# Two heads in 32 output rows, feature sums over two heads, key sums in PSUM, a shorter stage behind each chunk

## The reference

```python
h = rmsnorm(layernorm(x), norm_w);  q, k, v = h @ Wq, h @ Wk, h @ Wv          # 16 heads of 8
q_phi, k_phi = taylor(q @ Wqf), taylor(k @ Wkf)        # 1, 16 linear, 136 quadratic terms
# linear branch, chunks of 128 tokens with a running state (kv, ksum)
A = (qb . kb) * causal;  y = A @ vb + qb @ kv;  z = A.sum() + qb @ ksum;  lin = y / (z + 1e-6)
kv += kb.T @ vb;  ksum += kb.sum()
win = softmax(q . k / sqrt(8) over the last 65 tokens) @ v
x = x + (layernorm(x) + concat(lin, win) @ Wout)
# experts: top 2 of 8, weights by softmax of the two logits
x = x + sum_e combine[e] * (silu(g) * l) @ W3[e],   g, l from (xn @ W1[e]) * (xn @ W2[e])
```

## Time and profile before

| | |
|---|---|
| median of three runs | 486.39 us |
| the profiled execution | 485.23 us, its span 483.5 us |
| TensorE busy | 421.5 us, 87% |
| VectorE, ScalarE, GpSimd busy | 313.9, 215.2, 184.3 us |
| mean granted TensorE clock | 0.949 of 2.4 GHz |

### The profile page before, as it was taken

How to read it: one execution, slowest core, us unless ns; L and a number is a source line. 1 busy time by engine, 2 the same in 40 slices (tenths; PEclk the granted TensorE clock), 3 DMA queues, 4 the chain that set the end, 5 groups by cost and what they waited for, 6 DMA issues and landing times. The chain is left out here.

```text
span 483.5 us, 15295 instructions
## 1 busy us (share of the span) xinstructions
PE 421.5 (87%) x5093; PEld 294.4 (61%) x5093; DVE 313.9 (65%) x1289; ACT 215.2 (45%) x566; POOL 184.3 (38%) x320
## 2 busy tenths in 40 slices
PE   0887899999999999999999983299999999999930
PEld 0455677777777777777877762045555555555510
DVE  5475555777877778777787766446666666666614
ACT  1456455556455555555555540034444444434410
POOL 5254424435555455554545633202222222222220
PEclk9999899999999999999999995589999999999975
DMA  7548975445645555432222900211111111111008
GB/s 199 134 128 165 213 140 98 121 128 149 165 101 127 141 147 157 110 77 55 65 64 65 278 11 22 64 50 36 41 43 34 30 40 41 34 32 35 18 28 237
DMA packets 91630, 46.19 MB, mean 96 GB/s; under 512 B 56410, under 2 KB 89852, under 8 KB 91554
## 3 DMA queue, kind: packets, MB, share of 16 engines
q1 hardware_dynamic: 88562, 40.49, 34.3%
q0 software_dynamic: 2272, 4.46, 2.9%
q10 hardware_dynamic: 720, 0.26, 0.2%
HBM read 33.67 MB, written 11.98 MB: 94 GB/s over the span
## 5 line engine op out<-in xcount | busy, mean ns | idle before, releaser
L1303 POOL DMA_INDIRECT results<-qas,mrowid x39 | 38.3, 983 | 123.2 <-ACT qas L853 123.2
L1284 POOL TENSOR_SCALAR_AFFINE_SELECT amat<-amat 128x512 f32<-128x512 f32 x64 | 42.4, 662 | 100.2 <-ACT amat L793 99.6
L1076 DVE TENSOR_REDUCE mrow<-ps 128x4 f32<-128x512 f32 x64 | 44.0, 688 | 55.1 <-PE ps L585 55.1
L723 PE MATMUL ps<-wgl,rest 128*128 (+1 forms) x156 | 75.2, 605 | 2.9 <-DVE hT L1173 2.2
L806 ACT ACTIVATE pmat<-ps 128x512 f32<-128x512 f32 x64 | 38.2, 597 | 69.0 <-PE ps L640 69.0
L793 ACT ACTIVATE amat<-ps 128x512 f32<-128x512 f32 x64 | 38.2, 597 | 31.3 <-PE ps L597 31.3
L1173 DVE TENSOR_TENSOR hT<-ps,kv_tok 128x512 f32<-128x512 f32 x39 | 27.0, 691 | 26.6 <-PE ps L723 15.9
L723 PEld LDWEIGHTS ps<-wgl,rest 128*128 128x128 f32 x156 | 27.1, 193 | 25.5 <-issue 25.4
L708 PE MATMUL ps<-w,rest 128*128 (+1 forms) x78 | 41.9, 620 | 0.0
L640 PE MATMUL ps<-identb,mneg 128*128 128x128 bf16 x512 | 39.6, 220 | 0.0
L853 ACT ACTIVATE qas<-rest,mweight 128x128 f32<-128x128 f32 x39 | 15.7, 402 | 50.0 <-DVE rest L1190 50.0
(11 more groups left out here) (164 smaller groups left out, 921.7 us busy)
## 6 DMA issues: line engine op xcount, KB each, us to landing
qa_parts<-wgl SPq DMA_DIRECT2D x12, 256.0 KB, 3.5
ks<-k_parts SPq DMA_DIRECT2D x32, 96.0 KB
qas<-qa_parts SPq DMA_DIRECT2D x32, 96.0 KB
xin<-routed SPq DMA_DIRECT2D x39, 72.0 KB, 1.9
ks<-k_parts SPq DMA_DIRECT2D x32, 64.0 KB
qas<-qa_parts SPq DMA_DIRECT2D x32, 64.0 KB
w<-in_W SPq DMA_DIRECT2D x2, 1024.0 KB, 6.0
wgl<-in_Wg SPq DMA_DIRECT2D x2, 1024.0 KB, 6.1
```

The source lines that it names most:

```text
L723: t = mm(ps[:, GL, :], zxT[:, k % 2, s, :], rhs(wgl[:, bass.ds(e, 1), s, :]), start=(s == 0), stop=(s == 1))
L1076: v.tensor_reduce(mrow[:], ps[:, SQ, :].rearrange("p (a k) -> p a k", k=CH), AX.X, ALU.max).then_inc(max_done, 1)
L1284: q.affine_select(out=amat[:, u % 2], in_=amat[:, u % 2], compare_op=ALU.is_ge, fill=0.0, base=0, pattern=[[0, 4], [1, CH]], channel_multi ...
L1303: q.indirect_dma_start(results, bass.IndirectOffsetOnAxis(mrowid[:, m:m + 1], 0), yw[:, m, :], None, bounds_check=RESULTS - 1, oob_is_err= ...
```

## The change

Two heads h and h+4 of a group of eight now share 32 output rows: the tiles `v1` and `state` are laid out so that a read of 32 columns finds the first head's nine values at 0 and the second's at 16, and zeros elsewhere. Both heads' products are added in PSUM, so a bank takes two units. ScalarE copies it every second unit, `linT` and `winT` have half as many blocks, and four transposes in unit 0 of `post` bring back both branches (eight in two units before). The normalisation is one pass over 32 head slots; `Wout` is reordered on the host to fit.

The feature sums run as two matmuls over 256 columns (two heads at once) in place of four over 128. The key sums of a sequence stay in PSUM (144 columns of the KV bank) and accumulate there; VectorE masks them into one of two state tiles, one operation per unit. The last chunk of each sequence computes no key sums, key features or cross products.

`post` has its transposes of results in unit 1 and its projection in unit 2. Two passes follow the last chunk in place of three: routing of chunks 14 and 15 is done in unit 3 of the same pass as its logits. Waits by `settle` in the attention loop are gone. The core of the diff (old code as above where left out):

```diff
+SLOTW = 288
...
-        v1 = sb("v1", [CH, 2, 2, H, 32])
-        state = sb("state", [PR, H, 32])
-        sadd = sb("sadd", [PR, 4, UD])
+        v1 = sb("v1", [CH, 2, 2, 2, SLOTW])
+        state = sb("state", [PR, 2, 2, SLOTW])
...
-        linT = sb("linT", [128, 2, 4, CH])
-        winT = sb("winT", [128, 2, 4, CH])
-        zrec = sb("zrec", [CH, H])
-        att = sb("att", [CH, 2, H, HD])
+        linT = sb("linT", [128, 2, 2, CH])
+        winT = sb("winT", [128, 2, 2, CH])
+        zrec = sb("zrec", [CH, 2 * H])
+        att = sb("att", [CH, 2 * H, HD])
...
+        def slot32(tile, h, heads=1):
+            lo = 128 * (h // 4 % 2) + 32 * (h % 4)
+            return tile[:, h // 8, lo:lo + 32 * heads]
+        def values4(tile, u, lo, hi):
+            at = 144 * (u % 2)
+            return tile[:, u // 2, at:at + 128].rearrange("p (g f) -> p g f", f=32)[:, :, lo:hi]
+        def values16(tile, lo, hi):
+            return tile.rearrange("p a (r x) -> p a r x", r=2)[:, :, :, 0:128].rearrange("p a r (g f) -> p a r g f", f=32)[:, :, :, :, lo:hi]
+        def folded(c):
+            return c % (T // CH) != T // CH - 1, c - c // (T // CH)
...
+            def positions(r):
+                pe.wait_ge(r_member, r + 1)
+                mm(ps[:, TR, 384:384 + E], before[:], member[:], start=True, stop=True)
+                mm(ps[:, TR, 392:392 + E], ones[:], member[:], start=True, stop=True).then_inc(pos_ready, 1)
             def post(c, u, p):
...
                 if u == 0 and has[1]:
-                    pe.wait_ge(evac_done, UNITS * c)
...
+                    for k in range(2):
+                        nc.tensor.transpose(ps[:, TR, k * CH:(k + 1) * CH], linT[:, 1 - p, k, :], ident[:])
+                    for k in range(2):
+                        t = nc.tensor.transpose(ps[:, TR, (2 + k) * CH:(3 + k) * CH], winT[:, 1 - p, k, :], ident[:])
+                    t.then_inc(t_out, 1)
+                if u == 1 and (has[1] or has[2]):
...
+                if u == 3 and has[2] and c >= NC:
+                    if has[1]:
+                        pe.wait_ge(x1_ready, c)
+                    positions(c - 2)
...
-                for k in range(2):
-                    for par in range(2):
-                        t = mm(ps[0:PR, PHI, k * CH:(k + 1) * CH], sums[:, par, :], as_[:, p, 4 * u + 2 * k + par, :],
-                               start=par == 0, stop=par == 1)
+                for par in range(2):
+                    t = mm(ps[0:PR, PHI, 0:2 * CH], sums[:, par, :], as_[:, p, 4 * u + par:4 * u + par + 3:2, :],
+                           start=par == 0, stop=par == 1)
...
+                later, kf = folded(c)
...
+                    j, hf, pair = u // 2, u % 2, n // 2
+                    pe.wait_ge(v1_ready, c + 1)
+                    if later:
+                        pe.wait_ge(phik_ready, kf + 1)
+                        pe.wait_ge(cross_ready, kf + 1)
+                        if kf or u:
+                            pe.wait_ge(state_done, UNITS * kf + u)
+                        for k in range(2):
+                            hp = 4 * u + 2 * k
+                            lo = 144 * (u % 2) + 64 * k
+                            t = mm(ps[0:PR, KV, hp * UD:(hp + 2) * UD], phik[:, p, hp:hp + 2, :].rearrange("p h f -> p (h f)"),
+                                   v1[:, p, 1, u // 2, lo:lo + 64].rearrange("p (h f) -> p h f", f=32)[:, :, 0:UD],
+                                   start=c % (T // CH) == 0 and hp == 0, stop=True, skip_group_check=True)
+                        t.then_inc(kv_ready, 1)
...
-                    bank = OUT0 + u % 2
+                    bank = OUT0 + pair % 2
                     pe.wait_ge(phisq_done, n + 1)
-                    if not early or n > 1:
-                        pe.wait_ge(evac_done, n - 1)
-                    if not early or n > 3:
-                        pe.wait_ge(state_done, n - 3)
+                    if u % 2 == 0 and pair > 1:
+                        pe.wait_ge(evac_done, pair - 1)
+                    if c % (T // CH):
+                        pe.wait_ge(state_done, UNITS * folded(c - 1)[1] + u + 1)
+                    elif c:
+                        pe.wait_ge(state_zeroed, 1)
                     for k in range(2):
-                        t = mm(ps[64 * k:64 * k + 64, bank, 0:CH], state[:, 2 * (2 * u + k):2 * (2 * u + k) + 2, :].rearrange("p h f -> p (h f)"),
-                               phiq[:, u % 2, k, :], start=True, stop=False, skip_group_check=True)
+                        t = mm(ps[64 * k:64 * k + 64, bank, 0:CH], slot32(state[:, c % 2], 4 * u + 2 * k, 2),
+                               phiq[:, u % 2, k, :], start=u % 2 == 0, stop=False, skip_group_check=True)
                     t.then_inc(inter_done, 1)
                     pe.wait_ge(amask_ready, n + 1)
                     for g in range(4):
-                        mm(ps[32 * g:32 * g + 32, bank, 0:CH], v1[:, p, 1, 4 * u + g, :], amat[:, u % 2, g, :],
+                        mm(ps[32 * g:32 * g + 32, bank, 0:CH], slot32(v1[:, p, 1], 4 * u + g), amat[:, u % 2, g, :],
                            start=False, stop=True, skip_group_check=True)
...
                     for hh in range(8):
-                        g, s = hh % 4, hh // 4
-                        t = mm(ps[32 * g:32 * g + 32, bank, CH + s * WINDOW:CH + (s + 1) * WINDOW], v1[:, p, j, 8 * hf + hh, :],
-                               pmat[:, u % 2, hh, :], start=True, stop=True, skip_group_check=True)
+                        g, r = hh % 4, hh // 4
+                        at = CH + hf * WINDOW
+                        t = mm(ps[32 * g:32 * g + 32, bank, at:at + WINDOW], slot32(v1[:, p, j], 8 * hf + hh),
+                               pmat[:, u % 2, hh, :], start=False, stop=True, skip_group_check=True)
                     t.then_inc(out_ready, 1)
...
+                    if u % 2:
+                        bank, a = OUT0 + pair % 2, u // 2
+                        act.wait_ge(out_ready, n + 1)
+                        if c > 1:
+                            act.wait_ge(t_out, c - 1)
+                        nc.scalar.copy(linT[:, p, a, :], ps[:, bank, 0:CH])
+                        nc.scalar.copy(winT[:, p, :, a * WINDOW:(a + 1) * WINDOW],
+                                       ps[:, bank, CH:2 * CH].rearrange("p (k t) -> p k t", k=2)).then_inc(evac_done, 1)
...
+                if later:
+                    if kf:
+                        dve.wait_ge(cross_ready, kf)
+                        dve.wait_ge(phik_ready, kf)
+                    v.tensor_copy(u_tok[:, :, 1:UD], kv_tok[:, c, 0, :].rearrange("p (h d) -> p h d", h=H)).then_inc(us, 1)
+                for w in range(2):
+                    t = v.tensor_copy(values16(v1[:, p, w], 0, HD), kv_tok[:, c, 2 - w, :].rearrange("p (a r g d) -> p a r g d", a=2, r=2, g=4))
+                t.then_inc(v1_ready, 1)
+                if later:
+                    dve.wait_ge(us, kf * 2 + 1)
...
+                    dve.wait_ge(ut_done, kf + 1)
+                    v.tensor_tensor(phik[:, p, :, 0:UD], ut[:], u_tok[:], ALU.mult).then_inc(phik_ready, 1)
...
+                if u == 0 and has[1]:
+                    dve.wait_ge(t_out, c)
+                    v.tensor_tensor(z3, tr[:, :, HD:UD], epslin[:].rearrange("p (h a) -> p h a", a=1), ALU.add).then_inc(den_ready, 1)
+                    dve.wait_ge(den_ready, c)
+                    v.reciprocal(zrec[:], zrec[:]).then_inc(rec_ready, 1)
+                    dve.wait_ge(rec_ready, c)
+                    if c > 1:
+                        dve.wait_ge(t_cat, c - 1)
+                    v.tensor_tensor(att[:], tr[:, :, 0:HD], zrec[:].to_broadcast([CH, 2 * H, HD]), ALU.mult).then_inc(att_ready, 1)
+                if u == 0 and has[2]:
...
-                if u == 3 and (has[1] or has[2]):
+                if u == 0 and has[3] and c - 3 < NC - 2:
+                    weights_row(c - 3)
+                if u == 1 and has[3] and c - 3 < NC - 2:
+                    dve.wait_ge(cat_copied, c)
+                    places(c - 3)
+                if u == 2 and (has[1] or has[2]):
...
+                if u == 3 and has[2] and c >= NC:
+                    places(c - 2)
+                    weights_row(c - 2)
...
+                    def next_state():
+                        if not later:
+                            return
+                        dve.wait_ge(kv_ready, UNITS * kf + u + 1)
+                        if c:
+                            dve.wait_ge(inter_done, n - 3)
+                        v.tensor_tensor(values4(state[:, (c + 1) % 2], u, 0, UD),
+                                        ps[0:PR, KV, 4 * u * UD:4 * (u + 1) * UD].rearrange("p (h f) -> p h f", f=UD),
+                                        statemask[:].rearrange("p (h f) -> p h f", f=UD), ALU.mult).then_inc(state_done, 1)
...
+                if u == (2 if c == NC else 3) and has[3] and c - 3 < NC - 2:
+                    scatter_first(c - 3)
```

(43 more changed lines are left out.)

301 lines of the change are left out of this document (99 added, 202 removed).

## The result

The changed kernel takes 479.93 us (four runs, 479.06 to 480.37); the kernel before, run beside it, 485.86 (483.49 to 486.51). The ratio is 0.988, 95% interval 0.985 to 0.992. It is faster by 5.9 us, where 10.8 were forecast, and it lies above the range. The profiled execution took 480.37, its span is 478.6.

The account below looks back on a forecast made before the run. TensorE's own queue was taken to bound the loop. Transposes -7.35, key sums -2.8, feature sums and shared rows 0, tail -0.1 sum to -10.25 us, giving 475.6 us, with eight in ten for 471 to 479.2.

Parts of the forecast that it names:

- Bound by TensorE's own queue: Chunk loop: it costs what TensorE's queue costs, counted from start to start, 14.91 us a chunk before the change.
- Transposes, -7.35: Unit 1 of chunks 1 to 15 loses four `winT` transposes, 0.49 us each chunk: 7.35 us saved.
- Key sums, -2.8: Eight units in chunks 7 and 15 lose key sums: six save 0.45 us, two only 0.05, as `winT` is awaited.
- Feature sums, 0: Two matmuls of 256 columns for four of 128: same columns, no gain; bounds -6.9 and +1 us.
- shared rows, 0: Output rows shared by two heads: matmuls, widths and strips stay, adding onto written words costs nothing; 0 us.
- The first: Rival: the gap in the feature sums goes with the matmuls, 6.9 us more gained, 468.7 us; chance 0.10.
- the third rival: Window products adding onto shared rows stall, up to 0.2 us a unit, +12.8, giving 488.4 us; chance 0.03.
- Tail, -0.1: Chain from last unit to first expert load: gains and losses sum to -0.1 us, bounds -2 to +1.5.
- The inner range: Total time from the bounds of the tail and the strided operand: 472.5 to 478.2 us around the forecast.
- the one on GpSimd: GpSimd operations keep their lengths; the power stops waiting, the mask comes 1.1 us sooner, slack grows to about 0.75.
- the second rival: Unit 0: the eviction becomes the bound, `winT` or mask or normalisation later, giving 478.6 us; chance 0.13.

Follow-up runs that it names:

- f5: Kernel of e1 with chunk 12's second scatter, in the tail, made to wait for the loop's last copy; 473.31 us.
- f8: Kernel of e1 with an extra indirect scatter of 64 rows to spare memory in unit 3, behind the power; steady chunk 14.41 us.
- e1: Changed kernel with GpSimd's first scatter of a chunk issued in unit 2 instead of unit 3; 475.80 us.
- e4: Changed kernel with the feature sums as four matmuls of 128 columns again; 481.72 us.
- g1: Kernel of e1 with an extra indirect scatter of 128 full rows (144 words) to spare memory in unit 3; steady chunk 15.07 to 15.18 us.
- g2: Kernel of e1 with an extra indirect scatter of 128 rows of 16 words to spare memory in unit 3; steady chunk 15.07 to 15.19 us.
- g4: Kernel of e1 with an extra indirect scatter of 96 full rows to spare memory in unit 3; steady chunk 15.07 to 15.20 us.
- g5: Kernel of e1 with an ordinary DMA of 128 rows to spare memory in unit 3, behind a short select; steady chunk 14.41 to 14.79 us.

## Why the prediction was wrong, point by point

- **Bound by TensorE's own queue:** right, as far as it went. With the wait gone a steady chunk is 14.41 us; 14.91 - 0.49 was forecast.
- **Transposes, -7.35:** right. Four transposes take 0.49 (180.00 to 180.49), and adding four costs 0.48 to 0.49 a chunk.
- **Key sums, -2.8:** right within 0.2 once nothing else is late: chunk 7 takes 13.09 in f5 for 14.41, 1.32 for 1.4. In the changed kernel it takes 14.51, since a wait of 1.3 eats it.
- **Feature sums, 0, and shared rows, 0:** right. 0.31 us, and 182.54 to 182.91 = 0.37 for line 691, for 0.36. The first and the third rival are out.
- **Tail, -0.1:** -0.7 came, inside its bounds. I didn't test its parts. (The inner range's lower end, 472.5, doesn't follow from the bounds named with it: 475.6 less the tail's 1.9 is 473.7.)
- **The step that failed** is the one on GpSimd, with the sentence that held the second rival down: "nothing is put ahead of that copy". I worked out that the power would stop waiting and that the mask would come 1.1 us sooner, and booked it as slack. The same 1.1 us moves the scatter from beside the copy to 0.7 us ahead of it. I followed the scatter only to GpSimd's next operation, and not to the other engines during its 1.07 us. The copy had 0.09 us of slack, so that any delay there went into TensorE at once: 6.4 us in 12 waits up to the last window product, and 1.3 in the one behind it, where 0.35 in chunks 7 and 15 were forecast. The place, the idle time and nearly the time (478.6 for 479.9) were the second rival's; its reason, a late mask or a new order on ScalarE, wasn't.
- **Could the trace of before have told?** Not the price; it even spoke against one. It is one of the five profiles in which scatters hold nothing back: VectorE's maximum starts 0.58 behind the first scatter, on time, and ScalarE's square at 187.09, 0.98 behind the second, has its usual 0.46 of idle time.

```profile
184.77 0.69 DVE L1076 TENSOR_REDUCE mrow<-ps 128x4 f32<-128x512 f32 x1 [0.94 <-PE ps L585]
```

  But it had the warning: a copy with 0.09 us of slack and a 1 us operation of another engine that the change moves across it. That deserved more than 0.13.

Open: what decides whether an execution is of the one kind or the other. The four profiles f5 to f8 come from one chip, and the profiles e1 to e4, g1, g2, g4 and g5 from three others. So it may be the chip, but it may be something else that those four had in common. The changed kernel itself has no time in which nothing was held: its four runs (479.06 to 480.37) and the nine of e4 all lie far above the 473.8 that it would take with f5's loop (480.37 less 217.72 - 211.12 = 6.6, an estimate). The kernel before takes 484.91 beside the runs of chip 12 and 485.58 beside those of chip 9, so its own time shows neither kind, and the comparison with it stands. Nor is the hold complete where it occurs: g1 and g2 each have one exp that ends 0.62 us behind a scatter, on time. Why it happens is open too. TensorE's later starts are on time, which speaks for its signals being late and not its work, but no row shows a signal.

## What to carry to other kernels

When a change makes one engine earlier, follow each of its operations to its new time and write down what every other engine waits for during it, and not only what comes next on the same engine. Where a copy has under 0.1 us of slack, an operation moved across it is a rival with a real chance, even if no dependency ties the two. And where most of a gain is missing, look for the chunks in which it is not missing (here those where the scatter is over earlier): they name the cause before any run. When a run is to show that something has no effect, look first whether the effect is there at all in that same trace, at a place that the edit left alone. Three runs here look like answers, on the number of rows, on the bare ordinary DMA and on the last copy, and for that reason aren't.

## What the runs showed of the hardware

In nine of 14 profiles an indirect DMA of GpSimd with 96 or 128 rows, 0.95 to 1.07 us long and once per profile 1.23, held back the waits of ScalarE for TensorE. What was due within it started 1.25 to 1.75 us behind its start, mostly 1.26 to 1.55 (copy, square and exp alike); of 277 such scatters 3 have a wait that ends between 0.35 and 1.25. VectorE's maximum was held too (1.69 behind the scatter at 163.00). In the five other profiles the same scatters held next to nothing: a copy followed one by 0.60, squares by 0.97, exps by 0.76. In executions of the first kind an ordinary DMA (0.65 us) and a select (0.88 us) held nothing back. The price was 0.5 us a chunk, and moving the scatter one unit, without changing it, gave it back.

The Trainium skill, "Trainium Architecture — The Big Picture", section "What this means for kernel authors", names one pair of compute engines that contend on their way to SBUF, VectorE and GpSimd. Here TensorE and ScalarE, no such pair, lost 0.5 us a chunk by an operation of GpSimd (the copy 1.23 us behind the products for 0.65). Whether that is contention for SBUF at all, no run here shows.
